# A pipelined S4D + Hydra + FFN tower on one core: FFN columns in three even chunks, biases by accumulating DMAs, a new list order and a new prologue

## The reference, cut to what matters

```
h = s4d_kernel(x, ...)                      # 64 steps x 128 rows x 1024 columns
h = concat(cls_tok, h)                      # 129 rows
y = layernorm(h)                            # "attn" part, residual x_init = y
xmid = gelu(y @ w_down.T + b_down)          # 1024 -> 128
g = hydra(hydra(xmid))                      # conv, gated scans, norm, projections
a = sigmoid(gate1)
g = xmid + a * xmid + (1 - a) * g
h = h + (y + g @ w_up.T + b_up)
z = layernorm(h)                            # FFN part
out = h + z @ base_W.T + base_b + lora(z, softmax router of 15, 8 experts of rank 16) * 2
```

## Time and profile before

| | |
|---|---|
| median of 3 runs | 2334.94 us (2334.63 to 2346.7) |
| the profiled execution: its own time | 2339.94 us |
| its span (first to last instruction) | 2338.2 us |
| mean granted TensorE clock | 0.968 |
| PE busy, PE weight loads busy | 2161.3 us (92%), 1805.6 us (77%) |
| DVE, ACT, POOL busy | 1847.3 us (79%), 1528.2 us (65%), 1091.2 us (47%) |
| mean DMA traffic | 57 GB/s |

### The profile page before, as it was taken

One profiled execution on the slowest core, in us unless ns is written; L12 is line 12 of the kernel. 1 busy time (PEld: TensorE's weight loads), 2 busy tenths in 40 slices (PEclk: granted clock), 3 DMA queues, 4 the chain that ended last, 5 costly groups with the idle time before them and its releaser, 6 DMA issues.

```text
span 2338.2 us, 51899 instructions
## 1 busy us (share of the span) xinstructions
PE 2161.3 (92%) x14117; PEld 1805.6 (77%) x14117; DVE 1847.3 (79%) x4980; ACT 1528.2 (65%) x2921; POOL 1091.2 (47%) x1350
## 2 busy tenths in 40 slices
PE   1356799999999999999999999999999999999998
PEld 1245688888888888888888888888888888888776
DVE  6847688888888888888888888888888888888764
ACT  2546576766677766667666767666777666676652
POOL 2534355444455444455444554444554444554331
PEclk9756799999999999999999999999999999999999
DMA  4400122112222122221122221122211222211211
GB/s 92 117 29 24 35 64 64 42 54 63 63 63 61 35 61 63 63 63 48 47 63 63 63 63 40 55 63 63 63 58 36 63 63 63 63 47 47 69 39 33
DMA packets 90061, 132.61 MB, mean 57 GB/s; under 512 B 20379, under 2 KB 63559, under 8 KB 90006
## 3 DMA queue, kind: packets, MB, share of 16 engines
q1 hardware_dynamic: 79176, 125.60, 18.2%
q10 hardware_dynamic: 10830, 6.35, 1.1%
HBM read 55.17 MB, written 76.74 MB: 56 GB/s over the span
## 4 chain that ended last, share of the span: by engine, by line
issue 43%; PE 27%; POOL 9%; DVE 7%; ACT 6%; POOLq 1%; DVEq 0%; ACTq 0%; DMA 0%; SPq 0%
PE bank L1611 5%; PE bank L1512 5%; POOL CB L901 4%; PE bank L1567 3%; PE bank L1542 2%; DVE NF L1241 2%; ACT L1006 2%; POOL XD L852 2%; PE bank L1685 1%; PE bank L1669 1%; POOL RS L886 1%; PE bank L1544 1%; PE bank L1543 1%; POOL RS L865 1%; PE bank L1659 1%
## 5 line engine op out<-in xcount | busy, mean ns | idle before, releaser
L1512 PE MATMUL bank<-w_hi,XHI 128*128 128x512 f32 (+1 forms) x1560 | 622.9, 399 | 0.0
L1512 PE MATMUL bank<-w_lo,XHI 128*128 128x512 f32 (+1 forms) x1560 | 554.7, 356 | 0.0
L1512 PE MATMUL bank<-w_hi,XLO 128*128 128x512 f32 (+1 forms) x1560 | 554.4, 355 | 0.0
L1147 DVE SCALAR_TENSOR_TENSOR CX<-bank,cw,CX 128x252 f32<-128x252 f32 (+5 forms) x804 | 335.7, 460 | 61.8 <-ACT CX L944 61.6
L901 POOL TENSOR_TENSOR CB<-CB,CM 48x252 f32<-48x252 f32 (+5 forms) x402 | 292.7, 728 | 153.6 <-ACT CM L929 142.7
L1512 PEld LDWEIGHTS bank<-w_hi,XLO 128*128 128x128 f32 x1560 | 295.5, 189 | 46.9
L1512 PEld LDWEIGHTS bank<-w_lo,XHI 128*128 128x128 f32 x1560 | 296.8, 190 | 41.4
L1512 PEld LDWEIGHTS bank<-w_hi,XHI 128*128 128x128 f32 x1560 | 296.4, 190 | 41.2
L929 ACT ACTIVATE T<-bank 64x512 f32<-64x512 f32 x256 | 151.4, 592 | 261.1 <-PE bank L1601 256.5
L865 POOL TENSOR_TENSOR RS<-VE,half_neg 128x1 f32<-128x1 f32 x65 | 35.5, 546 | 369.9 <-DVE VE L1339 369.9
L892 POOL TENSOR_TENSOR RB<-m_gt,AS 128x512 fp32r<-128x512 f32 x134 | 164.9, 1231 | 56.8 <-DVE AS L1413 56.8
(11 more groups left out here) (295 smaller groups left out, 5332.5 us busy)
## 6 DMA issues: line engine op xcount, KB each, us to landing
carried<-T SPq DMA_DIRECT2D x65, 512.0 KB, 4.8
T<-carried SPq DMA_DIRECT2D x65, 512.0 KB, 3.9
out<-HB SPq DMA_DIRECT2D x129, 256.0 KB, 3.2
tables<-tab SPq DMA_DIRECT2D x8, 560.0 KB, 4.3
TB<-tables SPq DMA_DIRECT2D x64, 70.0 KB, 2.7
carried<-U SPq DMA_DIRECT2D x65, 64.0 KB, 3.6
XM<-carried SPq DMA_DIRECT2D x65, 64.0 KB, 4.8
XI<-in_x SPq DMA_DIRECT2D x128, 32.0 KB, 2.8
```

The source lines that it names most:

```text
L1147: inc(STT(CX[:, c, :, s:CS], src[:, :, 0:CS - s], cw[:, c, k:k + 1], CX[:, c, :, s:CS], ALU.mult, ALU.add), "conv")
L1512: ins = mm(bank[:, 0:c1 - c0], xs_[:, 1 - p, k, :], ws[:, k, c0:c1], start=(c0 == HID and k == 0 and n == 0), stop=(last == k and n == 2))
```

## The change

It has five parts.

1. The 1024 + 144 = 1168 output columns of the FFN are cut into 384, 384 and 400 instead of 512, 512 and 144. The 400 are two blocks of 128 columns of `base_W`, then the LoRA inputs and the router. Columns 384 to 511 of each `bO` bank get only the LoRA product, and a new DVE call `partial` adds the two blocks from `bR` to `HB`; `turn_h` waits for it, since it writes over them. The first LoRA matmul of each half is split in two (384 and 128 columns).
2. The four bias matmuls per body go. POOL issues two accumulating DMAs per body instead: `bias_base` adds `base_b` (broadcast) to `HB` in SBUF, `bias_up` adds `b_up` to `carried` in DRAM.
3. The factor of the gate is folded into `w_up` and `be1`, so `gated_a` goes. `layer_out` moves from DVE to ACT, `shift_1` and `shift_2` from DVE to POOL. POOL's `shift_none` goes: ACT writes that part of `W` itself, in a second copy.
4. The lists of all engines have a new order.
5. Prologue: the bias tiles and their four instructions go; the eight LoRA loads move from ACT's queue to SP's, ahead of the last six small loads; ACT's first Tanh stands ahead of its weight loads; the chain of small DVE operations is reordered and shortened; the tables and inputs of tiles 0 and 1 are loaded inside the prologue after chunk 1.

```
-                    small(bias_s[...])  (two)
+                sp: 8 x dma_start(st4[:, :, e, :], lora_B[e]...)   # before the wait on s_zero and six small loads
+                    if c == 1:   sp.wait_ge(s_kept[0], 16); loads of TB and XI for tiles 0, 1
-                for k, dst in enumerate((up_bias, base_bias)):   # pool
-                    link(TT(dst[lo, :], bias_s[lo, k, :], dst[lo, :].bitcast(F32), ALU.subtract))
+                act.wait_ge(s_first, 64)
+                act.activation(v["t0"][:, :], ldt[:, :], ACT.Tanh, scale=1.0 / 16).then_inc(s_tdt, 1)
                 for n in range(NS):
                     load(n)
...
+                    def bias_up():          # pool
+                        if B:
+                            t = i - 2
+                            wait_carry(pool, t, p)
+                            inc(pool.dma_start(row[:, 0:HID], b_up.unsqueeze(0).broadcast_to([P, HID]),
+                                               accum_op=ALU.add), "upb")
+                    def bias_base():        # pool
+                        if E:
+                            wait(pool, te, xh2=1)
+                            inc(pool.dma_start(HB[:, 1 - p, :], base_b.unsqueeze(0).broadcast_to([P, HID]),
+                                               accum_op=ALU.add), "baseb")
...
+                    def partial():          # dve
+                        if E:
+                            wait(dve, te, rt=1, baseb=1)
+                            cols = HB[:, 1 - p, :].rearrange("p (a b) -> p a b", a=2)[:, :, OB:HALF]
+                            inc(TT(cols, v3(bR[:, 0:REST], P), cols, ALU.add), "part")
...
-                                mm(bO[h][:, :], row_sel[:, :], base_bias[:, HALF * h:HALF * (h + 1)], start=True, stop=False)
-                            ffn(HALF * h, HALF * (h + 1), bO[h], range(a, b))
+                            ffn(OB * h, OB * (h + 1), bO[h], range(a, b))
-                            ins = ffn(HID, FW, bR, range(a, b), last=KC - 1)
+                            ins = ffn(2 * OB, FW, bR, range(a, b), last=KC - 1)
...
-                            wait(pe, te, hw=1)
+                            wait(pe, te, hw=1, part=1)
...
-                            mm(bO[h][:, :], HWS[:, 0, :], lb_hi[:, c], start=False, stop=False)
+                            mm(bO[h][:, 0:OB], HWS[:, 0, :], lb_hi[:, HALF * h:HALF * h + OB], start=False, stop=False)
+                            mm(bO[h][:, OB:HALF], HWS[:, 0, :], lb_hi[:, HALF * h + OB:HALF * (h + 1)], start=False, stop=False)
...
-                            mm(bT[:, :], row_sel[:, :], up_bias[:, c], start=True, stop=False)
```

More of the change, by code:

```diff
@@ L127, in build @@
         U = sb("U", [P, 2, 2, P])
+        XI = sb("XI", [P, 2, P])
+        TB = sb("TB", [P, 2, 2, NTAB])
+        x_in = [sem("x_in_even"), sem("x_in_odd")]
+        HCH = 16
+        tab = sb("tab", [P, 2, HCH, NTAB])
+        s_kept = [sem(f"s_kept{i}") for i in range(2)]
         banks = [keep.enter_context(nc.psum_tensor(f"bank{i}", [P, 512], F32)) for i in range(8)]
@@ L258, in _ @@
                 small(gate[:, :], gate1.broadcast_to([P, 1]))
+                n = pieces.index(("b", 0))
+                st4 = stage[n].rearrange("p (a e r) -> p a e r", a=KC, e=NE)
+                for e in range(NE):
+                    sp.dma_start(st4[:, :, e, :], lora_B[e].rearrange("(a p) r -> p a r", p=P)).then_inc(s_ld[n], 16)
                 sp.wait_ge(s_zero, 3)
@@ L409, in evacuate @@
                     act.wait_ge(s_wt, k + 1)
+                    if n >= 0 and pieces[n][0] == "u":
+                        act.wait_ge(s_gate, 1)
                     cols = banks[k % RING][:, 0:len(src) * m].rearrange("p (a b) -> p a b", b=m)
@@ L739, in body @@
                 def body(i, p):
-                    if isinstance(i, int) and i == 0:
-                        load_x(0, 0)
-                    if active(i, -1, CLS + 1) and not (isinstance(i, int) and i + 1 >= CLS):
+                    if isinstance(i, int) and i == 1:
+                        for k in range(2):
+                            sp.wait_ge(s_kept[k], 16 * NHT // HCH // 2)
+                    if active(i, -1, CLS + 1) and not (isinstance(i, int) and not 1 < i + 1 < CLS):
                         load_x(i + 1, 1 - p)
@@ L1034, in keep_y, with layer_out @@
                             copy(YT[:, :, :].rearrange("p a b -> p (a b)"), bZ[:, :], "yte")
+                    def layer_out():
+                        if G:
+                            wait(act, r, outp=1)
+                            wait(act, r - 1, pin=3)
+                            if D:
+                                wait(act, td, gt=1)
+                            copy(U[:, p, 1, :], bY[:, 0:P], "u2")
                     def keep_w():
@@ L1097, in body @@
                     keep_h(1, 0)
+                    keep_y()
                     keep_h(1, 1)
[L1099 removed]
+                    layer_out()
                     exp_router()
@@ L1377, in stats_2 @@
                             wait(dve, td, st2=2)
+                            wait(dve, td - 1, nm2=1)
                             apart(dve)
@@ L1512, in ffn @@
                                 ins = mm(bank[:, 0:c1 - c0], xs_[:, 1 - p, k, :], ws[:, k, c0:c1],
-                                         start=(c0 == HID and k == 0 and n == 0), stop=(last == k and n == 2))
+                                         start=(k == 0 and n == 0), stop=(last == k and n == 2))
                         return ins
```

388 lines of the change are left out of this document (195 added, 193 removed).

## The result

| | before | after |
|---|---|---|
| median | 2339.95 us (2334.63 to 2346.7, 4 runs) | 2369.53 us (2368.25 to 2372.79, 4 runs) |
| ratio | | 1.0124, 95% interval 1.0093 to 1.0155 |
| the profiled execution: own time, span | 2339.94, 2338.2 us | 2372.79, 2370.7 us |
| mean granted TensorE clock | 0.968 | 0.958 |
| first transpose of `XI` on PE | 119.59 us | 87.53 us |

Slower by 1.2%, where 2.7% faster was forecast. The two stages went opposite ways: the prologue gave 32 us, and 59 bodies at 1.0 us each took 58 back; the last 7 us of the 33 by which the two profiled executions differ lie in the ramp and the tail.

What follows compares the result with a forecast made beforehand. PE was taken as the bound, DVE and ACT just behind. 2340 - 44 (59 bodies at 0.75) - 3 (other bodies) - 16 (prologue) = 2277, median 2272 us; own case 2245 to 2295, range 2212 to 2312.

Steps and rivals of the forecast that it cites:

- PE's own work: FFN, bias and LoRA matmuls on PE: new chunks -0.65, bias matmuls -0.93, split LoRA +0.11, together -1.47 us per body.
- `mix` to `turn_y` (6.45): First part of a body: ACT's eight operations set turn_y's start at 6.45 us after mix instead of 6.61; PE waits 0.3.
- to `turn_h` (17.3): Body from mix to turn_h: DVE's list up to HW sets 17.3 us instead of 18.10, 0.5 behind PE.
- `turn_h` to the next `mix` (14.0): Last part of a body, across the seam: 13.94 us before, 13.8 by PE's work, 14.0 with a remaining wait of 0.2.
- DVE now does one `RF` and one `HB` ahead of the second `XLO`, so it begins about 0.4 later: At the seam: second XLO 0.4 us later, another 0.3 ahead of Mt; slack used up, PE waits some 0.2.
- the forecast of 31.3: Length of one FFN body after the change: 17.3 + 14.0 = 31.3 us, 0.75 less than before.
- The DMAs: POOL's two accumulating DMAs per body: issues in some 7 us of idle time, landing in 8 us, hidden, cost nothing.
- The shifts on POOL: shift_1 and shift_2 on POOL: some 0.2 us replacing operations of 0.12 on DVE, in POOL's idle time.
- The prologue: Before the loop: LoRA loads moved to SP bring DVE's third chunk 8 us forward, first tile's loads another 8: -16 us.
- the bound of -25: Prologue's far bound: -25 us if SP is fast with the LoRA loads and DVE's chain alone sets it.
- The first tile's wait: First tile's loads, 7.87 us of idle time on POOL, move inside the prologue: -8 us.
- The new order costs more than it hides: Rival: seam waits of 1 us, decay_sums waiting for POOL's second decays_back behind carry_h; body near 31.9, 2308 us; chance 0.15.
- POOL is held up: Rival: POOL's DMA issues take 5 us each, delaying add_bc(1), root_1, norm_1, turn_a(0): 118 us, 2390; chance 0.03.

Runs made afterwards that it cites:

- e6: Kernel after with both RF ahead of the first XLO in VectorE's list, and GpSimd's first RB waiting for both RF: 2293.85 us, ratio 0.9793.
- e5: Kernel after with one wait more: GpSimd's V (kernel_q) waits for VectorE's second RF of the tile before; 2306.91 us, ratio 0.9845.
- e7: Kernel before with VectorE's last six calls in the changed order (RF, final, XLO, RF, final, XLO): 2404.85 us, ratio 1.0260.
- e13: e6 with VectorE's router(7), partial, router(8), stats_2(1) to (3) ahead of softplus(4) and later ones, partial staying ahead of router(8): 2264.67 us, ratio 0.9664.
- e9: e6 with VectorE's router(7), router(8) and stats_2(1) to (3) ahead of partial and later softplus steps: 2303.10 us, ratio 0.9844.
- e1: Kernel after with both RF ahead of the first XLO in VectorE's list, as before the change: 2650.91 us, ratio 1.1327.
- e3: Kernel after without the two accumulating DMAs and their waits, both biases left out of the output: 2371.51 us, ratio 1.0129.
- e10: e6 without the two accumulating DMAs, both biases left out of the output: 2293.03 us, ratio 0.9800.
- e15: Kernel after with shift_2 alone back on VectorE, ahead of softplus(12): 2307.22 us, ratio 0.9839.
- e2: Kernel after with GpSimd's list as before at its ends (swap ahead of kernel_q, carry_h behind decays_back(1)): 2430.86 us, ratio 1.0380.

## Why the prediction was wrong

**PE's own work: right in its prices, its sum not reached.** Starts of FFN matmuls are 0.18 us apart (0.17 to 0.19 in the timeline). The price of LoRA's 128 columns can only be seen together with the next matmul, 0.34 us for both, which is 0.107 + 0.233. The four bias matmuls are gone. But PE's busy time per body went from 31.90 us to 30.96 (after) and 30.70 (e6), worked out from its 1591.33, 1498.53 and 1547.86 us in the window 400 to 2000 and the body of each. That is 0.9 to 1.2 less, where 1.47 was said. Busy time holds a little for each restart behind a wait; which calls take the rest no run tells.

**`mix` to `turn_y` (6.45) and to `turn_h` (17.3): right.** Medians are 6.41 and 17.25, and DVE's `HW` ends the wait at `turn_h`, 0.44 us in the mean, where 0.5 was said. These two terms held, and the mechanism with them.

**`turn_h` to the next `mix` (14.0): this step failed.** It took 15.8 us in the mean. Of the 1.8 us more, PE's waits are 1.4: it waits 0.48 for ACT at `turn_d`, 0.57 for `RF` and 0.51 for `Mt`, where 0.2 was said. Two terms were wrong.

The larger is `RF`. The prediction said of the seam that "DVE now does one `RF` and one `HB` ahead of the second `XLO`, so it begins about 0.4 later". It priced `RF` by its own length and not by what POOL does beside it. In its new place it falls on POOL's `RB` and `V`, and it takes 2.6 us; the second `XLO` starts at 1036.15, 1.6 us after its `XHI` is there (1034.55). e5 gives 1.08 us of the body back by one wait on POOL and nothing else, e7 puts 1.10 us on the kernel before by moving `RF`. So this is shown both ways. The trace of before already had the hint: `RF` took 1105 ns in the mean and from 677 to 1533 one by one. Beside an idle POOL it takes 684 (e13). The prologue of before had it twice more: two DVE operations of 128x128, 0.29 us each elsewhere, took 2.33 and 2.38 beside POOL's two of 2.47 and 2.34 on the bias tiles.

The smaller is the wait for ACT at `turn_d`, which the prediction put at nothing without a reason. `T` hangs on a chain of its own: DVE's `stats_2`, POOL's `root_2` and `shift_2`, then ACT. It starts 19.4 us after `mix` in the kernel after and started 19.7 after it before. PE gained more than these 0.3 us, and the difference is the wait, 0.48 us in the kernel after and in e6; 59 times that are 28 us. In e9 and e13, where the statistics stand further ahead in DVE's list, the wait is gone. It is what e6, whose body is 31.74 against the forecast of 31.3, has left of this step: `decay_sums` and `mix` no longer wait there.

Of this kind the Trainium skill says, in "SBUF — State Buffer", section "SBUF: two separate sides", that DVE instructions with two SBUF inputs and GpSimd instructions that read SBUF share a port pair which is an exclusive lock: who starts first has it for the whole instruction, the other waits. By that rule as I read it the held `RF` would wait for one instruction, `RB`, and end at 1034.7, and the body would be 32.1. The trace agrees with the exclusive turns (`RF` ends 0.6 us after a POOL instruction, the swap copy grows from 0.28 to 0.74, `XLO` with an input in PSUM stays at 683 ns), but `RF` waited for two instructions here and for five in e1. The prediction cited this section, but only for a DMA issued by POOL, which was no cost: the rule was at hand and was put to the wrong pair of instructions.

**The DMAs: right.** The accumulates land in 5.1 and 8.2 us (8 was taken), the issues take 0.95 and 1.10 us, in idle time. e3 and e10 measure them at nothing. The shifts on POOL were put at nothing too, since they lie in its idle time, and for `shift_2` that was wrong: with it back on VectorE (e15) the time is 2307.22 instead of 2369.53, since POOL's first `RB` then comes behind the first `RF` and the second `RF` is held for one instruction only.

**The prologue: right in its mechanism, half as large as it was.** -32 us instead of -16, and beyond the bound of -25. The term took 19.54 us for the LoRA issues, as on ACT; on SP the same eight took 8.21. The last small load was issued at 22.90, not 37.1, and had landed 1.6 us later, not 5.4. With that PE's first transposes stood at 24.46, not 42.5, and DVE's third chunk began at 32.28, not 50.4 (before: 58.45). The 18 us are the same in both places, so the chain was the one that the prediction named, and this stage gave 26 us instead of 8. The first tile's wait gave another 5.5 (10.43 to 4.88 of idle time on PE), where 8 was said.

**The rivals.** "The new order costs more than it hides" was the nearest, chance 0.15, but with a wait of 1 us for POOL's second `decays_back`. `decay_sums` did wait, for DVE's `RF`, and the price was above what the rival allowed. "POOL is held up" had the two engines the wrong way round: it was DVE that was held, by POOL. No case of mine had it, so the chance of 0.04 for slower was far too small: an engine's list had been moved past another's in 59 bodies, and I had only priced the instructions.

With the stall cured the change gives 2293.85 us (e6), and with one more reordering 2264.67 (e13). That e13 lies near the forecast of 2272 is luck: the prologue gives 16 us more than the sum had, and without them e13 would be at 2281 and e6 at 2310. The forecast left out two things: that `RF` is held, 63 to 76 us (e5 and e6 against the kernel after), and the wait at `turn_d`, about 28.

## What to carry over

Before an instruction is moved, look at what the other engine does at its new place. On VectorE and GpSimd that is a price of its own for each instruction with two SBUF inputs, and a mean duration above that of a like shape elsewhere in the trace is the sign. Where several of GpSimd's instructions follow each other, put the VectorE instruction ahead of the run and let the first of the run wait for it: a wait added to an engine with slack can be worth more than one removed.

## What was not expected of the hardware

**Several POOL instructions in a row can go ahead of a DVE instruction that waits.** 0.68 us became 2.6 (after), 2.7 (e7), 2.9 (e2) and 5.3 (e1). In other places turns alternate: in the kernel before and in e7, DVE's `NF`, asked for 0.4 us into POOL's `NB`, ends 0.6 us after it, and `WI`, which is next on POOL, takes 1.3 instead of 0.85 us.

**The clock makes a long wait longer.** In e1 PE is busy for 2.46 of 4 us and then for 0.28 of 2; of the idle time 2.79 us are one wait, ahead of the second half of `turn_d`. Windows around it (PE, PEld, DVE, ACT, POOL busy, granted clock, DMA share, GB/s):

```profile
1023.00:1027.00 4.00, 2.46 (x21) 2.25 (x20) 4.00 (x1) 2.24 (x5) 4.00 (x5) 1.00 0.00 0
1027.00:1029.00 2.00, 0.28 (x2) 0.29 (x3) 2.00 (x3) 0.00 (x0) 1.21 (x2) 0.86 0.00 0
1029.00:1031.00 2.00, 2.00 (x12) 2.00 (x11) 1.36 (x3) 1.11 (x2) 0.00 (x0) 0.50 0.00 0
1031.00:1033.00 2.00, 2.00 (x15) 1.86 (x16) 1.00 (x4) 1.13 (x2) 0.28 (x1) 0.50 0.86 203
1033.00:1035.00 2.00, 2.00 (x12) 2.00 (x11) 2.00 (x3) 0.07 (x1) 1.27 (x1) 0.50 0.88 238
1035.00:1037.00 2.00, 2.00 (x13) 2.00 (x12) 1.49 (x3) 1.98 (x4) 1.06 (x1) 0.93 0.99 373
```

Behind the wait PE is granted 0.50, its 1.2 GHz level, for some 6 us. From `turn_d(1)` to the first FFN matmul it needs 6.2 us (1028.7 to 1034.9), in e6 3.5 us. Neither stretch holds a wait. So of the 5.8 us by which e1's body is longer than e6's, about 2.7 are the clock's. The mean clock in e1's loop is 0.91, so this is no matter of one body.

**Accumulating DMAs.** 512 KB with an accumulate land in 5.1 us into SBUF and 8.2 us into DRAM, where a plain transfer of that size that SP issues takes 3.9. The two also have a broadcast source and another queue (POOL's), and which of these makes them longer was not tried.

**The same loads, another queue.** Eight strided DMAs took ACT 19.54 us to issue and SP 8.21. Why was not tried.
